# Sixteen weight chunks split in the first dense iteration and two per later one, in place of eight and three

## The chip, the core and the metric

The kernel runs on one core of a Trainium2 chip. The metric is device time in microseconds of one execution. The core has a matrix engine (PE in the profile, with its weight loads as PEld), a vector engine (DVE), a scalar engine (ACT), GpSimd (POOL) and a queue engine that mainly issues transfers (SP). Each runs its own instruction stream in order, and they meet at semaphores.

## What is computed

`x` holds 64 items of 64 tokens with 256 features. Two layers follow each other.

```
# layer 0: one adapter per item
h = gelu(x @ down_W.T + down_b)                     # 256 -> 64
h = h @ expert_W[id].T + expert_b[id] + domain_emb[id]
x = layernorm(h @ up_W.T + up_b + x)
# layer 1: normalise per token, then per item over its tokens, style by subject, two of 8 experts
h = item_norm(layernorm(x)) * gamma[subject] + beta[subject]
gates, idx = top_k(softmax(h @ router_w), 2)        # renormalised gates
y = sum over the two experts of gate * (relu(h @ w1[e] + b1[e]) @ w2[e] + b2[e])
out = x + y
```

The eight experts' `w1` (256 x 1024) and `w2` (1024 x 256) are float32 in memory. The kernel works with each weight as a sum of two float16 numbers, a high and a low part, times 256.

## The kernel before

It has two phases, `dense` and `experts`, one after the other. `experts` runs 39 tiles of gathered rows through the expert matmuls and needs all weights in their two float16 parts (`w_high`, `w_low`) in on-chip memory.

`dense` cuts the 4096 tokens into eight groups of 512 and runs ten iterations, `i.g` = 0 to 9, as a software pipeline: in iteration n the group n is in stage one (`s1`: transposed into features, down, adapter, up, all on PE with ACT copies), group n-1 in stage two (`s2`: the two layer norms of layer 0 and 1 on DVE, ACT and POOL), group n-2 in stage three (`s3`: item norm, router, splitting the rows in high and low parts) and group n-3 in stage four (`s4`: places in the expert queues and the scatter of the rows by POOL). Each engine has its own `body` with these steps in a fixed order, written out by hand, and no engine goes on to the next step before the one ahead is done.

The splitting of the weights is woven into the same iterations. The weights are 32 chunks of 128 x 1024. For a chunk three things happen:

- SP loads it (512 KB) into one of four buffers `stage` (line 364). It waits until the chunk four before it has been cut (`w_low_ready`, line 363).
- ACT makes the high part, `cut_high`, line 642. It waits for the load.
- DVE makes the low part, `cut_low`, line 911, from `stage` and `w_high`. It waits for ACT, and frees the buffer.

`CUTS` says how many chunks belong to each iteration. In iteration 0, ACT and DVE have a body of their own: chunks 0 to 4 stand between the four steps of `copy_selected`, and the rest of the iteration's chunks come in one run at its end, before either engine begins iteration 1:

```python
                        for b in range(SELECTS):
                            cut_high(i, slice(b + 1, b + 2))
                            copy_selected(b)
                        adapted(s1)
                        cut_high(i, slice(SELECTS + 1, None))
                        return
```

In the later iterations ACT makes its high parts at three places among the steps of stage one (the third takes all from the third chunk on), and DVE cuts all low parts of the iteration in one run after `norm_shift` (line 848) and before `best_two` (line 918). Behind that run come `their_experts`, the choice masks, `low` (line 943) and `row_fields`, and then the next iteration's `place_rows` and the moments of its stage two (line 821). `low` waits for `high` (ACT, line 681), which waits for PE's transposes back (line 570), which follow the router's matmuls (line 564); these wait for the item norm (ACT line 667, DVE line 900).

POOL's stream in an iteration: `rstd` of the first norm (lines 437, 439; waits for DVE's moments), three scatters (line 448), two power operations for the item norm (line 463; DVE's `item_scale` at line 880 waits for them), `rstd` of the second norm (DVE's `norm_shift` waits for it), five scatters.

SP's stream in an iteration: in iteration 1 first a store of spare rows and of queue padding, then the iteration's weight loads, then the load of x two groups ahead (waits for `up_done`), then the store of the finished rows `rb`. ACT and DVE wait in iteration 1 also for the small network that makes the style: DVE's `style_layer(1)` (line 792) stands behind its moments, PE's line 503 waits for it and stands ahead of PE's lines 529 and 534, and at the end ACT's `softplus` (lines 633 to 637) is followed by DVE's `item_gammas` (line 814).

Of the kernel before, what the change touches and what calls it, by code (L numbers as in the profile page):

```python
# [53 lines left out]
NONE_ROW = ADAPTERS  # L54
CHUNK = 1024
CHUNKS = 2 * EXPERTS * DC * FF // CHUNK
CUTS = [8, 3, 3, 3, 3, 3, 3, 3, 3, 0]
assert sum(CUTS) == CHUNKS and len(CUTS) == GROUPS + 2
W2_AT = EXPERTS * DC * FF
STAGES = 4  # L60
# [80 lines left out]
def dense(nc, sem, env):  # L141
# [10 lines left out]
    with ExitStack() as ctx:  # L152
# [185 lines left out]
        def chunks(i):  # L338


            start = sum(CUTS[:i.g])
            return [(q, q % STAGES, q // STAGES) for q in range(start, start + CUTS[i.g])]

# [1116 lines left out]
```

## Time and profile before

| | |
|---|---|
| median of 3 runs | 640.93 us (640.7 to 641.24) |
| profiled execution | 642.02 us, its span 640.2 us |
| PE, DVE, ACT, POOL busy | 85%, 63%, 43%, 39% of the span |
| mean granted PE clock | 0.876 of full speed |
| dense phase and tables | 0 to about 239 us of the span |
| expert phase | from about 239 us to the end |
| weight chunks | 32 loads of 512 KB; ACT 1.04 us and DVE 1.22 us for one |

The span is the profiler's time from the first to the last instruction; the execution's own time is 1.8 us longer. A time at a row below is counted from the start of the span. A row with "xN" merges N instructions that follow each other; its duration is theirs together. "idle before" names how long the engine stood still ahead of the row and what ended it.

### The profile page before, as it was taken

How to read it: one execution, taken by the hardware profiler on the slowest of the kernel's cores; microseconds unless marked ns; L12 is line 12 of the kernel's file. 1: busy time of each engine (PE TensorE's matmuls, PEld its weight loads, DVE VectorE, ACT ScalarE, POOL GpSimd, SP SyncE). 2: the span in 40 equal slices, each digit the busy share in tenths (PEclk: the TensorE clock that was granted, in tenths of full speed). 3: DMA queues.
4: the chain of work that ended last, by engine and by line, in shares of the span. 5: the costliest groups of instructions: out<-in, count | busy, mean ns of one | idle time of the engine just before them, and what ended most of it. 6: DMA issues, size and time to landing. Idle time of an engine off the chain costs nothing.

```text
span 640.2 us, 15839 instructions
## 1 busy us (share of the span) xinstructions
PE 542.2 (85%) x4370; PEld 461.7 (72%) x4371; DVE 402.6 (63%) x1431; ACT 278.0 (43%) x628; POOL 247.6 (39%) x208
## 2 busy tenths in 40 slices
PE   5986878888814308999999999999999999999992
PEld 4864665667614306888888888888888888888772
DVE  2566988998896534565656565656565655655571
ACT  2557656666643204343525343434434343434350
POOL 2010388778788520222323333323333323233221
PEclk8689778776865557999999999999999999999997
DMA  9363435565341244433333333333333424232321
GB/s 262 138 193 121 164 129 194 177 196 185 118 153 67 88 154 118 51 42 58 41 58 41 58 47 52 55 44 58 41 58 41 60 39 65 38 44 37 50 33 19
DMA packets 78082, 57.41 MB, mean 90 GB/s; under 512 B 51346, under 2 KB 71699, under 8 KB 77907
## 3 DMA queue, kind: packets, MB, share of 16 engines
q1 hardware_dynamic: 62610, 37.31, 21.4%
q0 software_dynamic: 13296, 17.83, 16.5%
q10 hardware_dynamic: 2146, 1.91, 1.2%
q8 instruction: 14, 0.23, 0.1%
q14 instruction: 16, 0.13, 0.1%
HBM read 23.18 MB, written 24.55 MB: 75 GB/s over the span
## 4 chain that ended last, share of the span: by engine, by line
PE 60%; DMA 1%; issue 1%; POOL 0%; ACT 0%; SPq 0%; DVE 0%; POOLq 0%; DVEq 0%
PE banks L1240 31%; PE banks L1256 29%; DMA out<-yg,token 1%; DMA rT<-queues 1%; POOL out L1205 0%; ACT yg L1304 0%; SPq L1177 0%; DVE yb L1373 0%; POOLq L1214 0%; DVEq L1373 0%; SPq L1179 0%; POOLq L84 0%
## 5 line engine op out<-in xcount | busy, mean ns | idle before, releaser
L1205 POOL DMA_INDIRECT out<-yg,token x71 | 117.0, 1648 | 287.3 <-ACT yg L1304 177.2
L1240 PE MATMUL banks<-rT,w_high 128*128 128x256 f16 (+1 forms) x1248 | 198.0, 266 | 23.9 <-DMA rT<-queues 23.4
L1240 PE MATMUL banks<-rT,w_low 128*128 128x256 f16 (+1 forms) x624 | 163.9, 265 | 0.0
L1256 PE MATMUL banks<-w_high,hid_high 128*128 x568 | 154.9, 273 | 0.8
L1256 PE MATMUL banks<-w_high,hid_low 128*128 x568 | 154.8, 273 | 0.0
L1256 PE MATMUL banks<-w_low,hid_high 128*128 x568 | 154.8, 273 | 0.0
L1288 ACT ACTIVATE hid<-banks,feat 128x256 f32<-128x256 f32 (+1 forms) x312 | 119.4, 455 | 65.6 <-PE banks L1240 52.9
L1240 PEld LDWEIGHTS banks<-rT,w_high 128*128 x1248 | 115.0, 98 | 43.0 <-issue 25.4
L1304 ACT ACTIVATE yg<-yb,gate 128x256 f32<-128x256 f32 x71 | 32.6, 501 | 186.0 <-DVE yb L1373 186.0
L1342 DVE TENSOR_TENSOR hid_low<-hid,hid_high 128x512 f16<-128x512 f32 (+1 forms) x156 | 101.1, 648 | 5.4
L1340 DVE CAST hid_high<-hid 128x512 f16<-128x512 f32 (+1 forms) x156 | 67.8, 434 | 45.4 <-issue 22.8
L1373 DVE SCALAR_TENSOR_TENSOR yb<-banks,b 128x256 f32<-128x256 f32 x71 | 27.2, 420 | 104.4 <-PE banks L1256 102.4
L448 POOL DMA_INDIRECT queues<-h_rows,slot x64 | 72.2, 1128 | 22.8 <-issue 17.4
L1240 PEld LDWEIGHTS banks<-rT,w_low 128*128 x624 | 61.4, 98 | 6.4
L1256 PEld LDWEIGHTS banks<-w_high,hid_high 128*128 128x128 f16 x568 | 55.6, 98 | 8.3 <-issue 1.9
L1256 PEld LDWEIGHTS banks<-w_low,hid_high 128*128 128x128 f16 x568 | 55.6, 98 | 6.4
L1256 PEld LDWEIGHTS banks<-w_high,hid_low 128*128 128x128 f16 x568 | 55.6, 98 | 6.3
L564 PE MATMUL banks<-rw,hT 128*128 128x8 f32 x128 | 21.5, 305 | 31.7 <-ACT hT L667 31.7
L564 PEld LDWEIGHTS banks<-rw,hT 128*128 128x128 f32 x128 | 21.1, 256 | 34.0 <-ACT hT L667 33.9
L911 DVE SCALAR_TENSOR_TENSOR w_low<-stage,w_high 128x1024 f16<-128x1024 f32 x32 | 37.8, 1228 | 2.8 <-ACT w_high L642 2.8
L667 ACT ACTIVATE hT<-hT,aff_c,aff_a 128x64 f32<-128x64 f32 x64 | 22.1, 427 | 33.8 <-DVE aff_c L888 33.8
L642 ACT ACTIVATE w_high<-stage 128x1024 f16<-128x1024 f32 x32 | 33.4, 1053 | 4.3 <-DMA stage<-expert_w 4.3
(179 smaller groups left out, 613.0 us busy)
## 6 DMA issues: line engine op xcount, KB each, us to landing
stage<-expert_w SPq DMA_DIRECT2D x32, 512.0 KB
xb<-x SPq DMA_DIRECT2D x8, 512.0 KB
out<-rb SPq DMA_DIRECT2D x8, 512.0 KB, 3.2
queues<-pad_row SPq DMA_DIRECT2D x5, 260.0 KB
out<-yg,token POOLq DMA_INDIRECT x71, 3.8
queues<-pad_row ACTq DMA_DIRECT2D x4, 260.0 KB
queues<-h_rows,slot POOLq DMA_INDIRECT x64
b<-exp_b SPq DMA_DIRECT2D x1, 1024.0 KB, 5.1
```

The costliest lines, as they stand in the source:

```text
L448: nc.gpsimd.indirect_dma_start(out=queues, out_offset=bass.IndirectOffsetOnAxis(ap=slot[:, i.par, t, k:k + 1], axis=0), in_=h_rows[:, i.pa ...
L564: last = nc.tensor.matmul(ps_lg[:, t, :], hT[:, c, t * P:(t + 1) * P], rw[:, c, :], start=(c == 0), stop=(c == DC - 1))
L642: nc.scalar.activation(w_high[:, bass.ds(q * CHUNK, CHUNK)], stage[:, slot], ACT.Copy, scale=WSCALE).then_inc(w_high_ready, 1)
L911: V.scalar_tensor_tensor(w_low[:, w], stage[:, slot], WSCALE, w_high[:, w], ALU.mult, ALU.subtract).then_inc(w_low_ready, 1)
L1205: nc.gpsimd.indirect_dma_start(out=out, out_offset=bass.IndirectOffsetOnAxis(ap=token[:, i.par, s:s + 1], axis=0), in_=yg[:, i.par, s, :], ...
L1240: last = nc.tensor.matmul(ps_in(i, c), w[:, at], features(i)[:, v, k, :], start=(n == 0), stop=(n == 3 * DC - 1))
L1256: last = nc.tensor.matmul(ps_out(i.par)[:, s, :], v[:, i.par, c, s * P:(s + 1) * P], w[:, at], start=(n == 0), stop=(n == 3 * FC - 1))
L1288: last = nc.scalar.activation(hid[:, c, 0:i.rows], ps_in(i, c), ACT.Relu, scale=1.0 / WSCALE, bias=feat[:, bass.ds(e * FC + (B1 + c), 1)])
L1304: nc.scalar.activation(yg[:, i.par, s, :], yb[:, s, :], ACT.Copy, scale=gate[:, i.par, s:s + 1]).then_inc(gated, 1)
L1340: V.tensor_copy(hid_high[:, i.par, s, r], hid[:, s, r]).then_inc(split_high, 1)
L1342: V.tensor_tensor(hid_low[:, i.par, s, r], hid[:, s, r], hid_high[:, i.par, s, r], ALU.subtract).then_inc(split_low, 1)
L1373: last = V.scalar_tensor_tensor(yb[:, s, :], ps_out(i.par)[:, s, :], 1.0 / WSCALE, b2[:, bass.ds(e * D, D)], ALU.mult, ALU.add)
```

## The change

One line: the numbers of chunks in each iteration. The total stays 32. Iteration 0 gets chunks 0 to 15 (before 0 to 7), iterations 1 to 8 two each (before three). Iteration 9 has none, as before. Nothing else in the source is touched; each engine's stream takes its chunks from `chunks(i)`, which reads `CUTS`.

```diff
 CHUNK = 1024
 CHUNKS = 2 * EXPERTS * DC * FF // CHUNK
-CUTS = [8, 3, 3, 3, 3, 3, 3, 3, 3, 0]
+CUTS = [16, 2, 2, 2, 2, 2, 2, 2, 2, 0]
 assert sum(CUTS) == CHUNKS and len(CUTS) == GROUPS + 2
```

## Rows read from the trace of the kernel before

**Rows 1.** Busy time per engine in stretches; last three: PE clock, DMA share, GB/s.

```profile
0.00:38.89 38.89, 29.99 (x135) 24.35 (x136) 16.98 (x28) 17.59 (x19) 3.52 (x25) 0.69 0.68 204
...
38.89:58.52 19.63, 15.29 (x79) 10.46 (x80) 12.14 (x38) 12.71 (x20) 2.55 (x4) 0.91 0.55 177
...
77.70:98.40 20.70, 16.70 (x83) 13.13 (x84) 17.93 (x85) 12.08 (x23) 16.10 (x13) 0.76 0.46 154
...
179.60:200.30 20.70, 7.30 (x40) 7.13 (x40) 17.82 (x83) 9.42 (x18) 17.16 (x15) 0.52 0.23 82
...
239.00:640.00 401.00, 384.27 (x3576) 338.33 (x3576) 229.31 (x695) 157.01 (x423) 117.00 (x71) 0.98 0.34 50
```

**Rows 2.** Timeline, end of iteration 0: start, duration, engine, line, operation, idle before.

```profile
30.21 1.24 DVE L911 SCALAR_TENSOR_TENSOR w_low<-stage,w_high 128x1024 f16<-128x1024 f32 x1
...
32.98 2.94 ACT L642 ACTIVATE w_high<-stage 128x1024 f16<-128x1024 f32 x3
...
34.05 3.50 DVE L911 SCALAR_TENSOR_TENSOR w_low<-stage,w_high 128x1024 f16<-128x1024 f32 x3 [2.48 <-ACT w_high L642]
...
38.89 1.43 DVE L821 BATCH_NORM_STATS2 stats<-banks 128x6 f32<-128x256 f32 x4 [1.34 <-PE banks L555]
...
39.84 1.08 ACT L649 ACTIVATE xT<-banks 128x512 f32<-128x512 f32 x2 [3.92 <-PE banks L517]
```

**Rows 3.** Timeline: the cut that frees the slot of the seventh load.

```profile
23.40 1.24 DVE L911 SCALAR_TENSOR_TENSOR w_low<-stage,w_high 128x1024 f16<-128x1024 f32 x1
```

**Rows 4.** Windows around loads into `stage`, columns as in rows 1.

```profile
9.00:17.00 8.00, 4.94 (x12) 1.92 (x12) 3.00 (x11) 2.34 (x2) 0.00 (x0) 0.57 1.04 386
...
25.50:27.25 1.75, 1.75 (x10) 1.75 (x9) 1.55 (x2) 1.55 (x2) 0.00 (x0) 0.50 0.86 297
...
36.25:39.75 3.50, 3.50 (x18) 2.76 (x17) 2.16 (x5) 0.00 (x0) 0.00 (x0) 0.86 0.83 282
```

**Rows 5.** Timeline: the same PE work in iterations 0 and 1, and iteration 1's end.

```profile
12.96 1.94 PE L529 MATMUL banks<-ident,item_add 128*64 128x512 f32 x2 [0.53 <-DVE w_high L777]
...
14.69 2.90 PE L534 MATMUL banks<-xT,dw 128*64 128x512 f32 x4
...
41.38 1.07 PE L529 MATMUL banks<-ident,item_add 128*64 128x512 f32 x2
...
42.29 1.88 PE L534 MATMUL banks<-xT,dw 128*64 128x512 f32 x4
...
57.93 0.29 DVE L814 SCALAR_TENSOR_TENSOR item_gamma<-w_high 128x128 f32<-128x128 f32 x1 [5.76 <-ACT w_high L637]
```

**Rows 6.** Timeline: `high` on ACT and `low` on DVE, iterations 2, 3, 7, 8.

```profile
74.24 1.02 ACT L681 ACTIVATE h_rows<-banks 128x1024 f16<-128x1024 f32 x1 [0.73 <-PE banks L570]
...
76.18 1.22 DVE L943 TENSOR_TENSOR h_rows<-banks,h_rows 128x1024 f16<-128x1024 f32 x1
...
95.67 1.02 ACT L681 ACTIVATE h_rows<-banks 128x1024 f16<-128x1024 f32 x1 [1.60 <-PE banks L570]
...
96.86 1.22 DVE L943 TENSOR_TENSOR h_rows<-banks,h_rows 128x1024 f16<-128x1024 f32 x1
...
176.27 1.02 ACT L681 ACTIVATE h_rows<-banks 128x1024 f16<-128x1024 f32 x1 [0.97 <-PE banks L570]
...
178.10 1.22 DVE L943 TENSOR_TENSOR h_rows<-banks,h_rows 128x1024 f16<-128x1024 f32 x1
...
198.93 1.22 DVE L943 TENSOR_TENSOR h_rows<-banks,h_rows 128x1024 f16<-128x1024 f32 x1 [0.51 <-ACT h_rows L681]
```

**Rows 7.** Timeline of POOL: scatters of iteration 3, starts of iterations 4 and 5.

```profile
91.86 2.10 POOL L448 DMA_INDIRECT queues<-h_rows,slot  x1 [0.18 <-issue]
...
96.42 0.96 POOL L448 DMA_INDIRECT queues<-h_rows,slot  x1 [0.30 <-issue]
...
100.31 0.22 POOL L437 TENSOR_SCALAR rs<-mv 128x4 f32<-128x4 f32 x1 [0.40 <-issue]
...
120.65 0.22 POOL L437 TENSOR_SCALAR rs<-mv 128x4 f32<-128x4 f32 x1 [1.50 <-DVE mv L826]
```

## The prediction, made before the changed kernel was run

> **What bounds the kernel now.** I read the page first (shares of the engines), then windows cut at the dense iterations, then the timeline of two iterations, then the waits of POOL and ACT. The windows show two different machines [rows 1]. From 239 us to the end PE is busy 384 of 401 us at clock 0.98: the expert phase is PE's, no weight chunk is split there, and the change can only shift it as a whole. In the dense phase an iteration such as 77.70 to 98.40 takes 20.70 us, of which DVE is busy 17.9; PE (16.7) and POOL (16.1) come close behind. Iteration 0 and iteration 1 are looser: DVE is busy 17.0 of 38.9 us and 12.1 of 19.6 us. What the change takes from the iterations and what it puts at the front are therefore priced separately, each by the wait that ends last there.
>
> **The run at the end of iteration 0.** It now holds chunks 5 to 15 in place of 5 to 7. Today DVE cuts 5, 6, 7 from 34.05 to 37.55, then stands idle 1.34 us until PE is through, and starts iteration 1 at 38.89 with line 821; ACT starts it at 39.84 after 3.92 us idle [rows 2]. The eight new chunks first fill that 1.34 us. Were all data there, they would take DVE 8 x 1.17 = 9.4 us (3.50 us for three [rows 2]) and end at 46.9. But they are not there: four buffers, and a load is issued only when the chunk four before is cut. So each load waits for this chain: chunk cut, load, ACT, DVE. How long is a load? The buffer of the seventh load is free when the cut at 23.40 ends, 24.64 [rows 3], and its bytes move until 27.25 [rows 4]: 2.6 us, with the signal about 2.7. With 1.04 us on ACT, 1.22 on DVE and 0.1 of lags that is 5.1 us for four chunks, 1.28 each, if transfers never collide. If they follow each other closely, bandwidth sets the pace. Two loads back to back took the 3.5 us from 36.25 to 39.75 at 282 GB/s; the start of the kernel, with many transfers queued, moved 386 GB/s for 8 us [rows 4]. For 524,288 bytes that is 1.86 and 1.36 us; I take 1.6 between them, since here two or three loads will be queued, more than in the one window and fewer than in the other.
>
> Step by step: chunk 4 is cut at 31.45 (30.21 + 1.24), so load 8 lands at about 34.2, before ACT is through with 5 to 7 at 35.92 [rows 2]. Load 9 is released by chunk 5's cut at 35.27 (34.05 + 1.22) and lands at 38.0. From there six more loads at 1.6 us: load 15 lands at 47.6, and 2.36 us later (ACT, DVE, lags) its cut ends, at 49.96. That is 11.1 us after 38.89. The bounds: without collisions chunk 9 is cut at 40.4 and chunk 11 at 42.8, load 15 lands 2.7 later and is cut at 47.9, +9.0 us; at 1.86 us a load the run ends at 51.5, +12.6.
>
> A page gives another price for the same thing. The Trainium skill's DMA: Bandwidth & Descriptors, Anatomy of one DMA, has a fit for GpSimd-issued transfers of 2.0 us plus bytes over 436 GB/s. It would give 3.2 us for a load alone and 1.2 us for each further one in a queue; the end of the drain would come to 48.7 us as an estimate from that page, and the whole forecast 1.3 us lower. By that rule, the traced load alone is shorter (2.7) and the traced pair slower (1.86 each at its rate) [rows 3, 4]; these loads are issued by SP, not by GpSimd.
>
> **What stands behind that run.** ACT's features of group 1 (line 649), DVE's moments and style layer 1, and with it PE's lines 503, 529 and 534. PE reads the style layer from DVE, so ACT's being ready a little before DVE gives nothing back. SP's stores of iteration 1, its loads 16 and 17 and the load of x for group 2 wait behind load 15's issue, but that issue comes when chunk 11 is cut, at about 44, and x is wanted only an iteration later: nothing. The adapter's and select's conditions on chunks 16 and up are long met: nothing.
>
> **PE's clock in iteration 1.** PE will have finished the transposes of group 1 soon after 39.84, where ACT's row on them begins [rows 2], and then wait some 11 us for DVE. In iteration 0 after such a pause (mean clock 0.57 from 9 to 17 us [rows 4]) lines 529 and 534 took 1.94 + 2.90 us; in iteration 1 before, at full clock (2.4 GHz), 1.07 + 1.88 [rows 5]. So up to 1.9 us more on a chain that iteration 1 waits for: adapter, up, transposes, softplus. Against it, iteration 1 today has some 3.5 us at half clock (mean clock 0.91 over 19.63 us [rows 1]: 0.09 x 19.63 / 0.5); if they fall elsewhere, up to 1.75 us come back; a longer one costs 1.0 more. I take +1.0 (0 to 2.9).
>
> **The chunk taken from iterations 1 to 8.** DVE saves 1.17 us in each, ACT 1.04. What of it reaches the end?
> Iteration 1: nothing. Behind its cuts DVE idles 5.76 us for ACT's softplus [rows 5].
> Iterations 2 to 8: behind the cuts stand the choice of experts and then `low`, and `low` needs `high` on ACT, which has just come from PE's transposes. The gap between `high`'s end and `low`'s start is all that DVE can move up [rows 6]. In iteration 2: 76.18 - 75.26 - 0.04 of signal = 0.88 us. In iteration 3: 96.86 - 96.69 - 0.04 = 0.13. It grows over the next four, to 0.77 in iteration 7; the five from 3 to 7 add up to 2.7. In iteration 8 `low` already waits 0.51 us for `high`: 0. Together 3.6 us.
> Of the chunks' 8 x 1.17 = 9.4 us, then, 5.8 turns into a wait of DVE for ACT's `high`. Where PE's clock is higher than in this trace `high` comes earlier and the saving can reach the full 1.17 for iterations 2 to 7.
>
> POOL is the next limit. At 100.31 its first operation of iteration 4 follows the last scatter by 0.40 us of pure issue: no slack; at 120.65 it had waited 1.50 for DVE, 1.1 more than that 0.40 [rows 7]. Iteration 7 is like 3, iterations 4, 5, 6 like the second. But scatters that meet a cut take 2.10 us instead of 0.96 [rows 7], 1.1 more, and I expect a scatter that lies under the third cut to give 0.9 of it back when that cut is gone. So POOL allows 0.9 in iterations 3 and 7 and 1.1 in 4 to 6, more than `high` does. At the most then 1.17 + 2 x 0.9 + 3 x 1.1 = 6.3 us. Downwards I allow 2.2, which is what is left if PE's slow stretches fall worse in two of the six.
> The Trainium skill's SBUF — State Buffer (SBUF: two separate sides; Who interferes with whom) says that DVE and GpSimd share a port pair as an exclusive lock, for a DVE instruction with two SBUF inputs only against a GpSimd operation that reads SBUF, and it infers that writing descriptors is spared; spared scatters would mean rival (3) below. By that rule, 2.10 beside 0.96 speaks for a block.
>
> **Sum.** +11.1 (run at the front) + 1.0 (clock) - 3.6 (saved) = +8.5 us. The profiled execution has a span of 640.2 and took 642.02, 1.1 above the median of 640.93; I put the sum on the median: 649.4 us, a profiled span near 648.7.
>
> **Rivals.** What tells a change from none here is about 0.2%, 1.3 us.
> (1) Mild: the drain runs at the chain's own pace (+9.0), clock costs nothing, savings are 6.3: +2.7, 643.6 us. For it: 386 GB/s was reached. Against: the pair at 282 GB/s and the gate at `high` [rows 4, 6]. Cases between +1.3 and +5.5: chance 0.17.
> (2) Heavy: loads at 1.86 us and PE half-clocked through iteration 1: +12.6 + 2.9 - 2.2 = +13.3, 654.2 us. For it: the nearest row for paired loads. Cases above +11.5: 0.14.
> (3) POOL keeps the beat: the scatters get nothing back from the missing cut, iterations 3 and 7 save nothing, and 0.88 + 1.80 = 2.7 us are left: +9.4, 650.3 us. For it: POOL's zero slack at 100.31; against: the long scatter lies exactly under a cut [rows 7]. Chance 0.2, inside the main case's.
> (4) The other side, one mechanism: iteration 1 absorbs the delay. DVE idles 5.76 us there [rows 5]; if the start of iteration 1 on DVE could be late by that without making softplus late, the front would cost 11.1 - 5.8 = 5.3, and with savings of 6.3 and no clock cost the kernel would take 1.0 less, 639.9, or 3.1 less at the lower drain. It decides once absorption and saving together pass the drain's 9.0 to 12.6. Against: softplus is at the end of a chain that begins with DVE's style layer and ACT's features, both behind the run. Faster by over 0.2%: 0.03; within 0.2%, by this or by (1) at its extreme: 0.04.
> That the change does nothing can't be: the counts fix the streams.
> Main case, +5.5 to +11.5: 0.62. A bound under all but (4): DVE's own work in the run costs 46.9 - 38.9 = 8.0 even with all data there, and the iterations give back at most 6.3. Range 644 to 654, which leaves out the ends of (1) and (2).
>
> **What the profile will show.** Right: DVE's line 821 of iteration 1 near 50 us instead of 38.89, ACT and DVE waiting between the cuts of chunks 9 to 15 for `stage`, loads back to back there; iterations 2 to 7 shorter by 0.1 to 0.9 us with new idle time of DVE ahead of line 943, ended by ACT line 681; iteration 1 a little longer at a lower clock; the expert phase of the same length. Wrong: the eight cuts at DVE's own 1.2 us pace, or at 2 us and more; iterations shorter by 1.2 us throughout, with no wait at line 943; iteration 1 shorter by several us; a new wait of POOL or PE in the steady iterations.

## The result, and the profile after

The changed kernel takes 655.36 us (median; 653.11 to 657.84) where the kernel before, on the same chip, takes 640.82 (638.36 to 641.24): a ratio of 1.024, 95% interval 1.018 to 1.029. That is 14.5 us slower. The forecast was 8.5 slower, with 654 as the end of its range; the direction was right and the size was not.

The two profiled executions differ by a little more: span 655.9 against 640.2, 15.7 us. I compare these two, stretch by stretch. First windows of the changed kernel, columns as in [rows 1]: iteration 0, iteration 1, and the expert phase.

```profile
0.00:52.78 52.78, 31.19 (x144) 25.38 (x145) 26.60 (x36) 26.91 (x29) 3.53 (x25) 0.69 0.72 227
52.78:75.25 22.47, 16.86 (x69) 10.33 (x70) 11.21 (x38) 10.80 (x17) 2.55 (x4) 0.74 0.35 114
...
258.00:655.90 397.90, 383.31 (x3574) 337.71 (x3572) 228.71 (x695) 157.25 (x423) 121.51 (x71) 0.98 0.35 50
```

Iteration 0 ends at 52.78 instead of 38.89. Iteration 1 is 22.47 us long instead of 19.63, at a mean clock of 0.74 instead of 0.91, although it holds one chunk less. Iteration 3, also with one chunk less, is longer than before: 21.28 us (20.68 before). An iteration is counted here and below from DVE's start of line 821 on `banks` to the next; iteration 8 ends with the start of line 958, iteration 9 with that of line 1056. The last stretch is the same machine as before: PE busy 383 of 398 us at 0.98. Where the 15.7 us went, by these starts:

| part | forecast | profiled pair |
|---|---|---|
| iteration 0 (start of line 821 in iteration 1) | +11.1 | +13.9 (38.89 to 52.78) |
| iteration 1 | +1.0 | +2.8 (19.63 to 22.47) |
| iterations 2 to 8 | -3.6 | -1.9 (141.77 to 139.90) |
| iteration 9, tables, expert phase | 0 | +0.8 |
| sum | +8.5 | +15.7 |

The last line has nothing of the change in it: iteration 9 takes 19.54 us against 19.52, and from its end to the end of the span it is 421.2 against 420.4, in a stretch whose instructions the edit leaves as they were. In the seventeen profiles of this case that last length lies between 419.1 and 422.0 us, with no order by the counts of chunks, so 0.8 is scatter.

All three terms have the right sign, and all three missed on the same side. How far one pair of profiles can be trusted is seen from the others: iteration 1 starts at 52.8 to 53.6 us in the seven profiles with sixteen chunks at the front, four buffers and SP's order unchanged, and at 38.89, 39.95 and 40.11 in the three with eight. The middle values differ by 13.2 us; the 13.9 of this pair has the earliest start before in it.

Now the end of iteration 0 in the changed kernel, from the timeline; what answers to [rows 2]. ACT first, then DVE.

```profile
33.05 3.88 ACT L642 ACTIVATE w_high<-stage 128x1024 f16<-128x1024 f32 x4
38.83 1.06 ACT L642 ACTIVATE w_high<-stage 128x1024 f16<-128x1024 f32 x1 [1.90 <-DMA stage<-expert_w]
41.09 1.06 ACT L642 ACTIVATE w_high<-stage 128x1024 f16<-128x1024 f32 x1 [1.20 <-DMA stage<-expert_w]
42.37 1.06 ACT L642 ACTIVATE w_high<-stage 128x1024 f16<-128x1024 f32 x1 [0.23 <-DMA stage<-expert_w]
43.65 1.06 ACT L642 ACTIVATE w_high<-stage 128x1024 f16<-128x1024 f32 x1 [0.22 <-DMA stage<-expert_w]
45.51 1.06 ACT L642 ACTIVATE w_high<-stage 128x1024 f16<-128x1024 f32 x1 [0.81 <-DMA stage<-expert_w]
48.04 1.06 ACT L642 ACTIVATE w_high<-stage 128x1024 f16<-128x1024 f32 x1 [1.47 <-DMA stage<-expert_w]
50.55 1.06 ACT L642 ACTIVATE w_high<-stage 128x1024 f16<-128x1024 f32 x1 [1.46 <-DMA stage<-expert_w]
...
34.13 4.63 DVE L911 SCALAR_TENSOR_TENSOR w_low<-stage,w_high 128x1024 f16<-128x1024 f32 x4 [2.49 <-ACT w_high L642]
39.92 1.23 DVE L911 SCALAR_TENSOR_TENSOR w_low<-stage,w_high 128x1024 f16<-128x1024 f32 x1 [1.16 <-ACT w_high L642]
42.17 3.79 DVE L911 SCALAR_TENSOR_TENSOR w_low<-stage,w_high 128x1024 f16<-128x1024 f32 x3 [1.03 <-ACT w_high L642]
46.60 1.23 DVE L911 SCALAR_TENSOR_TENSOR w_low<-stage,w_high 128x1024 f16<-128x1024 f32 x1 [0.64 <-ACT w_high L642]
49.12 1.22 DVE L911 SCALAR_TENSOR_TENSOR w_low<-stage,w_high 128x1024 f16<-128x1024 f32 x1 [1.30 <-ACT w_high L642]
51.64 1.22 DVE L911 SCALAR_TENSOR_TENSOR w_low<-stage,w_high 128x1024 f16<-128x1024 f32 x1 [1.29 <-ACT w_high L642]
52.78 1.41 DVE L821 BATCH_NORM_STATS2 stats<-banks 128x6 f32<-128x256 f32 x4
```

Read it as a ladder. After the first four chunks (5 to 8) each of ACT's rows was released by a load, so its start is the moment at which that load was there: 38.83, 41.09, 42.37, 43.65, 45.51, 48.04, 50.55. The last six steps take 11.72 us, 1.95 each. Against the release, a load takes 3.5 us at first (chunk 5 is cut at 35.3, chunk 9's load is there at 38.83) and 5.9 at last (chunk 11 is cut at 44.65, chunk 15's load is there at 50.55). DVE adds its five waits up to 5.4 us, and all of them are named ACT, which in turn waited for the DMA.

### The profile page after: what moved, and what is told of

It reads as the page before. It is cut to its first block, busy times and chain, and to the rows that moved or that the text cites. A ratio compares the mean times of both kernels' runs of the same rounds, so it can differ in the third digit from the quotient of the medians.

```text
span 655.9 us, 15839 instructions
## 1 busy us (share of the span) xinstructions
PE 539.0 (82%) x4370; PEld 459.1 (70%) x4371; DVE 404.0 (62%) x1431; ACT 279.3 (43%) x628; POOL 247.3 (38%) x208
## 4 chain that ended last, share of the span: by engine, by line
PE 54%; DMA 4%; issue 1%; DVE 1%; POOL 0%; ACT 0%; DVEq 0%; ACTq 0%; POOLq 0%; SPq 0%
PE banks L1240 28%; PE banks L1256 26%; DMA out<-yg,token 3%; DMA rT<-queues 0%; POOL out L1205 0%; DVE yb L1373 0%; DVE hid_high L1340 0%; ACT yg L1304 0%; DVEq L1170 0%; SPq L1177 0%; ACTq L1170 0%; ACT hid L1288 0%; DVE hid_low L1342 0%; DVEq L84 0%; POOLq L84 0%
## 5 line engine op out<-in xcount | busy, mean ns | idle before, releaser
L1205 POOL DMA_INDIRECT out<-yg,token x71 | 121.5, 1711 | 283.7 <-ACT yg L1304 170.4
L448 POOL DMA_INDIRECT queues<-h_rows,slot x64 | 69.7, 1088 | 24.2 <-issue 17.4
L564 PE MATMUL banks<-rw,hT 128*128 128x8 f32 x128 | 23.7, 322 | 36.5 <-ACT hT L667 36.5
L564 PEld LDWEIGHTS banks<-rw,hT 128*128 128x128 f32 x128 | 23.0, 278 | 39.0 <-ACT hT L667 39.0
L437 POOL TENSOR_SCALAR rs<-mv 128x4 f32<-128x4 f32 x16 | 6.7, 418 | 89.6 <-DVE mv L826 89.6
```

Of the source, the lines that this page charges most:

```text
L448: nc.gpsimd.indirect_dma_start(out=queues, out_offset=bass.IndirectOffsetOnAxis(ap=slot[:, i.par, t, k:k + 1], axis=0), in_=h_rows[:, i.pa ...
L564: last = nc.tensor.matmul(ps_lg[:, t, :], hT[:, c, t * P:(t + 1) * P], rw[:, c, :], start=(c == 0), stop=(c == DC - 1))
L1205: nc.gpsimd.indirect_dma_start(out=out, out_offset=bass.IndirectOffsetOnAxis(ap=token[:, i.par, s:s + 1], axis=0), in_=yg[:, i.par, s, :], ...
```

## The experiments

Each is the changed kernel with one edit, if nothing else is said. Ratios are to the kernel before on the same chip, with their 95% intervals.

**The two halves of the change apart.** The first kernel keeps the sixteen at the front and gives iterations 1 to 4 their three chunks back, with one each left for 5 to 8. The second leaves the front at eight, keeps two in iterations 1 to 8, and puts the eight that are left over into iteration 9.

```diff
-CUTS = [16, 2, 2, 2, 2, 2, 2, 2, 2, 0]
+CUTS = [16, 3, 3, 3, 3, 1, 1, 1, 1, 0]   # front sixteen
+CUTS = [8, 2, 2, 2, 2, 2, 2, 2, 2, 8]    # thin without front
```

> Counts 16, 3, 3, 3, 3, 1, 1, 1, 1, 0: the long first run kept, iterations 1 to 4 as before. Theory (front): the run ends near 52.8 us as in the changed kernel (38.9 before), iteration 1 takes about 22.5 us (19.6 before) because PE is at half clock after its wait; time 652 to 657 us. Rival (thin iterations): if a third chunk costs iterations 2 to 4 its whole 1.17 us, they are longer by that than in the changed kernel, in sum 3.5 us over 3 iterations; if PE's clock rules them, their lengths scatter by up to 2 us either way with no such difference.

> Counts 8, 2, 2, 2, 2, 2, 2, 2, 2, 8: the run at the front as before, the steady iterations thin, the eight chunks in the last iteration. Theory (front): line 821 of iteration 1 at 38.9 us, iteration 1 19.6 us long, iterations 2 to 8 together 1 to 4 us shorter than before, the last longer by the eight cuts' 9.4 us less the 3.9 us DVE waits there for the router; time 641 to 645 us. Rival (the extra time is in the thin iterations): they are no shorter, or longer, and iteration 1 is long with a short front too; time over 646 us.

Front sixteen: 655.2 us, ratio 1.0244 (1.0199 to 1.0289), the same as the change. Iteration 1 starts at 53.41 and takes 22.48 us with three chunks, as long as with two: the chunk that the change takes from iteration 1 is worth nothing there, as forecast, and iteration 1 became longer through the front alone. Iterations 2 to 4, with three chunks, take 59.4 us together against 59.1 with two in the changed kernel, and 5 to 7, with one, 57.9 against 60.2: in these two executions the third chunk cost 0.3 us in three iterations, and not the 3.5 that it is on DVE. Thin without front: iteration 1 starts at 40.11 and takes 17.94, and iterations 2 to 8 together 138.93, 2.8 less than before. But it took 654.69 us, 1.0223 (1.0172 to 1.0274), where 641 to 645 was expected, because iteration 9 grew from 19.52 to 34.51 us. Timeline of that iteration, ACT's fifth chunk:

```profile
213.81 1.06 ACT L642 ACTIVATE w_high<-stage 128x1024 f16<-128x1024 f32 x1 [12.98 <-DMA stage<-expert_w]
```

ACT waits 13 us for a load that could not be issued: DVE's first cut of the iteration ends at 208.8 us, SP issues the load then, and ACT's next steps stand behind it. With four buffers that DVE frees only late in an iteration, the fifth chunk of one has to wait like this; the kernel with five in iteration 1, below, shows it too. So this kernel is no clean sum, but its parts carry the reading: no cost in iteration 1, 2.8 us of savings in this execution.

**Fewer at the front.** Twelve in place of sixteen.

```diff
-CUTS = [16, 2, 2, 2, 2, 2, 2, 2, 2, 0]
+CUTS = [12, 3, 3, 3, 3, 2, 2, 2, 2, 0]
```

> Counts 12, 3, 3, 3, 3, 2, 2, 2, 2, 0: half of the change. Theory (the first extra chunk is free in DVE's wait, each further one costs the pace of its load, 1.3 to 2.5 us): line 821 of iteration 1 at 44 to 46 us (38.9 before, 52.8 with sixteen), time 645 to 650. Rival (the run costs by its loads' latency once, not by chunk): it starts at 49 us or more with four extra chunks as well.

649.2 us, 1.0093 (1.0060 to 1.0126). Iteration 1 starts at 45.91, 7.0 us late for four more chunks; the first 1.34 us were free [rows 2], so 8.4 us for four, 2.1 a chunk; sixteen chunks pay (13.9 + 1.3) / 8 = 1.9 a chunk. Iteration 1 takes 22.47 us here too: the whole price of that iteration is there after half of the delay. The time is inside what was expected (645 to 650), and the rival, a latency paid once, would have had the start at 49 or later.

**What makes the run at the front slow: stores or buffers.** SP's queue holds, at the head of iteration 1, a store of spare rows and one of padding. Timeline of SP in the changed kernel; the first row are loads 8 to 15:

```profile
31.54 13.50 SPq L364 DMA_DIRECT2D stage<-expert_w  x8
45.09 0.43 SPq L380 DMA_DIRECT2D out<-hT  x1
45.56 0.43 SPq L382 DMA_DIRECT2D queues<-pad_row  x1
```

Both stores are issued behind load 15, but loads 14 and 15 are on their way then. In this kernel they are issued after the loads of iteration 1 and the load of x; in the next one `stage` has six buffers; the third does both.

```diff
                 def body(i):
-                    if i.g == 1:
-                        sp.wait_ge(cleared_zero, 1)
-                        sp.dma_start(spare_rows, zero_out).then_inc(spare_stored, 16)
-                        sp.wait_ge(rows_numbered, 2)
-                        sp.dma_start(queues[IDLE:IDLE + SLOTS].rearrange("(s p) d -> p s d", p=P),
-                                     bcast(pad_row[:].bitcast(U32), 1, [P, SUB, ROW // 2])).then_inc(filled, 16)
                     load_weights(i, slice(STAGES if i.g == 0 else 0, None))
                     if (s2 := back(i, 1)) is not None:
...
+                        if i.g == 1:
+                            sp.wait_ge(cleared_zero, 1)
+                            sp.dma_start(spare_rows, zero_out).then_inc(spare_stored, 16)
+                            sp.wait_ge(rows_numbered, 2)
+                            sp.dma_start(queues[IDLE:IDLE + SLOTS].rearrange("(s p) d -> p s d", p=P),
+                                         bcast(pad_row[:].bitcast(U32), 1, [P, SUB, ROW // 2])).then_inc(filled, 16)
                         sp.wait_ge(x1_ready, s2.g + 1)
```

```diff
-STAGES = 4
+STAGES = 6
```

> The changed kernel with the store of the spare rows and the queue padding (388 KB) issued after the load of x for group 2 instead of straight behind load 15. Theory (these stores hold up loads 14 and 15, which landed 2.5 us apart against 1.3 before them): the run ends 1 to 2.5 us earlier, near 51 us, and so does the kernel. Rival (the loads' own pace and latency set the run's end): it ends within 0.4 us of 52.8.

> The changed kernel with six buffers in stage instead of four. Theory (the run at the front waits for loads, because a load is only released by the cut four chunks before it): with six released ahead, the loads follow at the 386 GB/s of a full queue, 1.36 us each, DVE ends its run near 49 us instead of 52.8, the time falls by 3 to 5 us. Rival (bandwidth): the loads come no faster than 1.9 us each also with more of them queued; the run ends within 1 us of 52.8.

> The changed kernel with six buffers and with the stores of iteration 1 behind the load of x. Theory (what keeps the front's run from DVE's own pace is only the load's wait for a buffer and these stores): the run ends at 47 to 48 us, against 48.5 with six buffers alone, 46.9 at DVE's own pace, and 52.8 in the changed kernel; 648 to 651 us. Rival (the bytes' bandwidth is a floor of its own): 48.5 or later.

Timelines of DVE, first with the stores behind, then with six buffers (and there one row of ACT), each from the first cut of the run to the moments of iteration 1:

```profile
34.70 4.63 DVE L911 SCALAR_TENSOR_TENSOR w_low<-stage,w_high 128x1024 f16<-128x1024 f32 x4 [2.47 <-ACT w_high L642]
...
52.07 1.42 DVE L821 BATCH_NORM_STATS2 stats<-banks 128x6 f32<-128x256 f32 x4
```

```profile
34.27 9.17 DVE L911 SCALAR_TENSOR_TENSOR w_low<-stage,w_high 128x1024 f16<-128x1024 f32 x8 [2.47 <-ACT w_high L642]
44.30 1.23 DVE L911 SCALAR_TENSOR_TENSOR w_low<-stage,w_high 128x1024 f16<-128x1024 f32 x1 [0.86 <-ACT w_high L642]
46.06 2.50 DVE L911 SCALAR_TENSOR_TENSOR w_low<-stage,w_high 128x1024 f16<-128x1024 f32 x2 [0.54 <-ACT w_high L642]
48.48 1.42 DVE L821 BATCH_NORM_STATS2 stats<-banks 128x6 f32<-128x256 f32 x4
...
41.12 1.06 ACT L642 ACTIVATE w_high<-stage 128x1024 f16<-128x1024 f32 x1 [1.17 <-DMA stage<-expert_w]
```

The run of eleven cuts takes 18.65 us in the changed kernel (34.13 to 52.78), 17.37 with the stores behind (34.70 to 52.07), 14.21 with six buffers (34.27 to 48.48), and 13.83 with both (34.67 to 48.50). By these traces the stores cost 1.3 us with four buffers and 0.4 with six, and the missing buffers 4.4. The same run takes 18.1 to 19.2 us in the seven profiles with four buffers and the stores ahead, so 1.3 can be 0.8 to 1.9, 4.4 can be 3.9 to 5.0, and 0.4 is less than the scatter. With six, eight cuts follow each other at DVE's own pace, and DVE's waits shrink from 5.4 us to 1.4. What the two buffers give is mostly a head start: the first load for which ACT waits in the run is chunk 12's at 41.12, where it was chunk 9's at 38.83; from there to chunk 15's (46.25) the three steps are 1.7 us each, not much under the 1.95 of the changed kernel. In time: 651.61 us, 1.0178 (1.0138 to 1.0218); 650.92, 1.0154 (1.0108 to 1.0200); 651.62, 1.0154 (1.0100 to 1.0208). These intervals overlap each other and that of the change, so the order of the causes is read from the traces and not from the times. Two expectations were missed: with the stores behind, the run ended at 52.07 and not near 51, between theory and rival, and with both edits at 48.50 and not by 48, so that a pace of the transfers beyond buffers and stores is not excluded. Even with every load in time, eleven cuts are 12.9 us of DVE, and eight of them are new: that part no buffer removes.

**PE's clock in iteration 1.** PE stands idle for 14.75 us in the changed kernel before line 503. Timeline of the changed kernel, PE and then DVE; what answers to [rows 5]:

```profile
54.92 0.66 PE L503 MATMUL banks<-w_high 128*128 128x64 f32 x2 [14.75 <-DVE w_high L792]
55.51 1.97 PE L529 MATMUL banks<-ident,item_add 128*64 128x512 f32 x2
57.27 3.62 PE L534 MATMUL banks<-xT,dw 128*64 128x512 f32 x4
...
65.14 1.06 PE L554 MATMUL banks<-uw,dom 65*128 65x256 f32 x2
...
68.59 0.59 PE L555 MATMUL banks<-xb,ident 128*128 128x256 f32 x2
...
61.11 0.28 DVE L798 TENSOR_SCALAR w_high<-banks,ab 64x64 f32<-64x64 f32 x1 [2.65 <-PE banks L503]
61.31 1.39 DVE L821 BATCH_NORM_STATS2 stats<-rb 128x6 f32<-128x256 f32 x4
...
74.66 0.29 DVE L814 SCALAR_TENSOR_TENSOR item_gamma<-w_high 128x128 f32<-128x128 f32 x1 [6.83 <-ACT w_high L637]
```

And DVE before, at the same place:

```profile
44.54 1.39 DVE L821 BATCH_NORM_STATS2 stats<-rb 128x6 f32<-128x256 f32 x4
```

Lines 529 and 534 take 1.97 + 3.62 us in place of 1.07 + 1.88: 2.64 more. The next instruction of PE is the style network's third layer (line 503), and DVE waits 2.65 us for it, where it did not wait before. So DVE reaches its second moments (line 821 on `rb`) 8.53 us after the start of the iteration instead of 5.65, and from there to the end it is 13.94 us against 13.98: the whole loss stands ahead of that line. DVE's wait for ACT's softplus at the end is 6.83 us instead of 5.76 because there is one cut less in front of it. Two kernels give PE work of no use for the wait, 27 and 54 matmuls into a bank that nobody reads.

```diff
                         into_features(s1)
                         if i.g == 1:
+                            for _ in range(27):   # 54 in the second
+                                nc.tensor.matmul(banks[:, 7, 0:P], ident[:], ident[:], start=True, stop=True)
                             style_layer(2)
```

> The changed kernel with 27 more matmuls of the identity by itself on PE, whose result is overwritten, between the transposes of group 1 and line 503, where PE otherwise stands still for about 14 us. Theory (clock): lines 529 and 534 take 1.1 and 1.9 us again instead of 2.0 and 3.6, iteration 1 takes 19.6 to 20.5 us instead of 22.5, the time falls by 1.5 to 3 us. Rival (order): iteration 1 is longer for another wait; it stays at 22 us or more.

> As the run with 27 more matmuls, which ended 6.6 us before PE was wanted again, but with 54, so that PE works on to about 55 us. Theory (clock): lines 529 and 534 take 1.1 + 1.9 us instead of 2.0 + 3.6, iteration 1 falls from 22.5 us to 20.5 or less. Rival (order): both lines stay at half clock or iteration 1 stays above 22 us.

With 27 the work ended at 48.69 and left PE idle for 6.6 us again; it took 655.78 us, 1.0211 (1.0140 to 1.0283), and decides nothing. With 54 (108 instructions in the profile), the timeline of PE, and two windows with the columns of [rows 1]:

```profile
40.83 12.22 PE L612 MATMUL banks<-ident 128*128 128x128 f32 x108
...
55.90 1.97 PE L529 MATMUL banks<-ident,item_add 128*64 128x512 f32 x2
57.66 2.47 PE L534 MATMUL banks<-xT,dw 128*64 128x512 f32 x4
...
53.00:55.00 2.00, 0.05 (x1) 0.00 (x0) 1.97 (x10) 0.66 (x2) 0.00 (x0) 1.00 0.94 348
55.90:57.70 1.80, 1.80 (x4) 0.56 (x4) 1.69 (x6) 0.00 (x0) 0.60 (x1) 0.50 0.02 8
```

PE worked until 53.05, 2.3 us before line 503. The granted clock was still full (1.00) in that pause, where in the changed kernel it was 0.50 from 44 us on, and yet it was 0.50 under line 529, which took 1.97 us as without the matmuls: what was expected, 1.1 and 1.9 us for the two lines, did not come. 655.37 us, 1.0194 (1.0149 to 1.0238). Iteration 1 was 19.59 us long here, but not, as far as the runs tell, for the reason that I had put into the kernel: line 534 and the up projection (lines 554 and 555, 3.7 us instead of 5.4) were faster, and the same shorter iteration came in kernels whose PE stream in iteration 1 is that of the changed kernel. Over all profiles but that of the kernel with five chunks in iteration 1: where the front was long, iteration 1 took 22.4 to 22.5 us in six executions with the up projection at 5.4, one of them the changed kernel profiled again, and 19.6 to 20.2 in five with 3.7; where the front was short, 19.63 twice with 5.4 and 17.9 to 18.0 three times with 3.7. Split at DVE's second moments, the two parts come apart. The first takes 5.65 us with a short front, 8.4 to 8.6 with a long one in the six and 7.3 to 7.9 in the five. The second takes 13.9 to 14.0 us with the up projection at 5.4 and 12.3 with 3.7, whatever the front. So the long front costs iteration 1 some 2.8 us at the one and 1.6 to 2.3 at the other, all of it in the first part, and the clock under the up projection makes another 1.6 to 1.7, which falls one way or the other without the change.

> The changed kernel once more, for one more trace. Theory (whether the half-clock stretch falls into line 554 and 555 of iteration 1 differs from run to run, and makes the two groups of times, 653 and 657 us): if this run takes 652 to 654 us, iteration 1 is 19.6 to 20.2 us long with 3.7 us in lines 554 and 555; if it takes 656 to 658, 22.5 us with 5.4. Rival: the time and iteration 1's length go apart.

The changed kernel again: 659.6 us, one execution; iteration 1 starts at 53.57 and takes 22.40, iterations 2 to 8 take 141.19. The long iteration goes with the long time, as the theory has it, though the time is above the 656 to 658 that I had expected.

**PE's clock in iterations 2 to 8.** First the changed kernel at the gate that the forecast named; timeline of iteration 3:

```profile
106.60 3.59 PE L564 MATMUL banks<-rw,hT 128*128 128x8 f32 x16 [3.32 <-ACT hT L667]
107.44 2.43 DVE L911 SCALAR_TENSOR_TENSOR w_low<-stage,w_high 128x1024 f16<-128x1024 f32 x2
...
110.04 1.95 PE L570 MATMUL banks<-ident,hT 128*128 128x128 f32 x8
...
110.46 0.37 DVE L918 MAX8 top<-lg 128x8 f32<-128x8 f32 x4 [0.59 <-ACT lg L674]
...
112.03 1.02 ACT L681 ACTIVATE h_rows<-banks 128x1024 f16<-128x1024 f32 x1 [1.60 <-PE banks L570]
113.08 1.23 DVE L943 TENSOR_TENSOR h_rows<-banks,h_rows 128x1024 f16<-128x1024 f32 x1 [0.58 <-ACT h_rows L681]
```

DVE is through with its two chunks at 109.87, waits 0.59 us for the router's logits ahead of the choice of experts, and then another 0.58 for `high`; both had waited for PE. The first of these waits is one that the forecast did not have; it is there in iterations 3, 5 and 7 (0.59, 0.68, 0.94 us). What decides is how long PE takes for the router and the transposes back:

| iteration | 2 | 3 | 4 | 5 | 6 | 7 | 8 |
|---|---|---|---|---|---|---|---|
| lines 564 + 570 before, us | 2.9 | 4.8 | 4.6 | 4.4 | 4.3 | 4.2 | 5.5 |
| after, us | 3.0 | 5.5 | 4.1 | 5.5 | 3.6 | 5.2 | 5.5 |
| length before | 19.19 | 20.68 | 20.34 | 20.32 | 20.34 | 20.24 | 20.66 |
| after | 18.09 | 21.28 | 19.68 | 20.83 | 18.86 | 20.51 | 20.65 |

Iterations 2, 4 and 6 save 1.1, 0.7 and 1.5 us; 3, 5 and 7 lose 0.6, 0.5 and 0.3, and they are the ones where PE spends 0.7 to 1.1 us more on these two lines. That is one draw. In seven profiles of kernels with sixteen chunks at the front and two in each later iteration, and with PE's work from iteration 2 on as in the changed kernel, iterations 2 to 8 take 137.7 to 142.1 us in sum, 140.3 in the middle, and 3 to 7 take 99.0 to 103.3; before, they took 141.8 and 101.9. Three kernels put useless matmuls of the same kind ahead of them. The first has eight ahead of the router in each iteration. The second has four to six at three places of iterations 3 to 7. The third is the kernel before with the same.

```diff
                 def route_and_back(i):
+                    pe.wait_ge(act_ready, upto(i.g, 3, GROUPS))
+                    for _ in range(8):
+                        nc.tensor.matmul(banks[:, 6, 0:P], ident[:], ident[:], start=True, stop=True)
                     pe.wait_ge(h_ready, i.g + 1)
                     pe.wait_ge(h_rest_ready, i.g + 1)
-                    pe.wait_ge(act_ready, upto(i.g, 3, GROUPS))
```

```diff
+                def keep_busy(g, n):
+                    for _ in range(n if g >= 3 else 0):
+                        nc.tensor.matmul(banks[:, 4, 0:P], ident[:], ident[:], start=True, stop=True)
...
+                    keep_busy(i.g, 4)
                     pe.wait_ge(act_ready, i.g + 1)
...
+                    keep_busy(i.g, 5)
                     pe.wait_ge(dom_ready, i.g + 1)
...
                 def route_and_back(i):
+                    keep_busy(i.g + 2 if i.g + 2 < GROUPS else 0, 6)
```

> The changed kernel with eight more matmuls of the identity by itself in each iteration ahead of the router's matmuls (line 564), while PE waits for the item norm; their result is overwritten. Theory (at half clock lines 564 and 570 take 5.5 us instead of 3.0, and that holds high, low and so the whole iteration): at full clock in more iterations, iterations 2 to 8 shorten by 2 to 5 us in sum. Rival (the clock is no limit there): their lengths stay, 139.9 us in sum, whatever lines 564 and 570 take.

> The changed kernel with 15 more matmuls of the identity by itself in each of iterations 3 to 7, four ahead of line 546, five ahead of line 554, six ahead of line 564, all where PE waits; their result is overwritten. Theory (PE's half clock, in line 554 and 555 or in 564 and 570, sets how long a thin iteration is): where both groups run at full clock (3.7, 1.95 and 1.1 us) an iteration takes 18.1 to 18.6 us, and iterations 3 to 7 sum to 93 or less instead of 101.2. Rival (another wait): they stay near 20 us each whatever PE's clock.

> The kernel before (8, 3, 3, ...) with the same 15 matmuls in iterations 3 to 7. Theory: at full clock DVE's own chain rules, the third chunk costs its 1.1 us, iterations 3 to 7 sum to 97 to 99 us (101.9 before, and 5 us above the thin ones); the kernel takes 3 to 5 us less than before. Rival (the third chunk is hidden under PE also then): thick and thin iterations are equal within 1 us in sum.

Eight ahead of the router: 654.76 us, 1.0206 (1.0147 to 1.0265). In iterations 2 to 7 the router ran at full speed (1.9 us) and the transposes at or near it (1.1 to 1.7), but iterations 2 to 8 took 139.1 us, hardly less than 139.9, where 2 to 5 us less was expected: the half-clock stretch had gone to the up projection in some iterations, 6.95 us in iteration 4 where full clock makes it 3.7, and made the router late. Three places, with the counts changed (first row, of 93.83 to 190.41, iterations 3 to 7) and with those of before (second row); windows, columns as in [rows 1]:

```profile
93.83:190.41 96.58, 87.48 (x576) 70.60 (x575) 84.23 (x408) 58.72 (x111) 78.62 (x70) 0.92 0.45 153
```

```profile
78.19:180.06 101.87, 89.25 (x578) 70.84 (x576) 89.63 (x411) 64.81 (x117) 80.52 (x69) 0.89 0.53 172
```

With two chunks, the five iterations take 96.6 us instead of the 101.2 of the changed kernel (93 or less was expected; the lowest without these matmuls is 99.0), and the time falls to 651.83 us, 1.0132 (1.0094 to 1.0170). With three, they take 101.9, exactly as before without the matmuls (97 to 99 was expected), and the time is that of before: 641.56, 0.9995 (0.9975 to 1.0016). So a faster PE was worth nothing with three chunks, and 0.9 us an iteration with two (0.5 to 1.3 by the spread above). With three, DVE is busy 89.6 of 101.9 us, and in the timeline of that third kernel (iteration 5) its two larger waits are for POOL:

```profile
128.17 0.17 DVE L887 TENSOR_TENSOR aff_a<-rsT,item_gamma 128x8 f32<-128x8 f32 x1 [1.17 <-POOL rsT L463]
...
132.72 0.16 DVE L855 SCALAR_TENSOR_TENSOR shift<-mv,rs 128x4 f32<-128x4 f32 x1 [0.94 <-POOL rs L439]
```

DVE's work and these answers of POOL set the length there (lines are seven further down in that kernel than in the profile of before, 880 and 848 there). With two chunks PE's router and transposes set it, if they run at half clock. At the higher clock (0.92 and 0.89 of full speed in these windows) a chunk is worth (101.9 - 96.6) / 5 = 1.06 us, nearly DVE's whole 1.17.

**Chunks where DVE waits anyway.** Iteration 1 has DVE idle for 5.8 us, iteration 9 has no chunk, and the front has 1.34 us free. Three kernels use these.

```diff
-CUTS = [16, 2, 2, 2, 2, 2, 2, 2, 2, 0]
+CUTS = [9, 5, 2, 2, 2, 3, 2, 2, 2, 3]   # where DVE waits
+CUTS = [9, 3, 3, 2, 3, 2, 3, 2, 2, 3]   # spread
+STAGES = 6                              # the third: spread, and six buffers
```

> Counts 9, 5, 2, 2, 2, 3, 2, 2, 2, 3: one more chunk than before in iteration 0 (DVE's 1.34 us wait), two more in iteration 1 (5.76 us wait), three in iteration 9 (3.9 us wait), two in most others. Theory (a chunk is free where DVE waits for another engine and costs its load's pace in a run of its own): iteration 1 starts at 38.9 to 39.5 us, is 19.6 to 20.5 long, iteration 9 no longer than 20, the steady ones 2 to 5 us shorter in sum; time 636 to 640 us, faster than both. Rival (the loads with four buffers set the pace wherever the chunks stand): iteration 1 and 9 grow by 2 us or more each, and the time is that of before or above.

> Counts 9, 3, 3, 2, 3, 2, 3, 2, 2, 3: one more in iteration 0 and three in iteration 9, where the run before showed no cost, four fewer in the steady iterations, iteration 1 as before (five chunks there made it 24.4 us). Theory: start of iteration 1 within 1 us of before, iteration 1 17.9 to 19.7, iteration 9 19.6, iterations 2 to 8 1 to 3 us shorter; time 1 to 3 us under before. Rival (the length of the iterations is PE's clock's, whatever DVE has to cut): within 1 us of before.

> Counts 9, 3, 3, 2, 3, 2, 3, 2, 2, 3 with six buffers. Theory (in these counts no cut waits for a load on the way that ends last): same as with four buffers within 1.5 us, 638 to 641 us. Rival (loads still hold something up): 2 us or more faster than with four.

Where DVE waits: 644.73 us, 1.0031 (1.0012 to 1.0050). Three chunks in iteration 9 cost nothing (19.56 us long, 19.52 before), but five in iteration 1 made it 24.38 us in place of 19.63, and the time missed the expected 636 to 640. Timeline of ACT in that iteration, in this kernel and then before:

```profile
51.60 1.06 ACT L642 ACTIVATE w_high<-stage 128x1024 f16<-128x1024 f32 x1 [4.75 <-DMA stage<-expert_w]
52.56 2.06 ACT L687 ACTIVATE nb<-rb,shift,rs 128x256 f32<-128x256 f32 x4
```

```profile
48.02 2.07 ACT L687 ACTIVATE nb<-rb,shift,rs 128x256 f32<-128x256 f32 x4 [0.37 <-DVE shift L848]
```

ACT waits 4.75 us for the fifth chunk's load. Its buffer is free only when DVE has made its first cut of the iteration, at 47.4 us, and ACT's layer norm (line 687), from which the chain to softplus goes on, stands behind it: it starts 15.4 us into the iteration, where before it was 9.1. The up projection ran at 3.7 us here, so the fair comparison is with the 17.95 us of the short iterations above: the two chunks cost 6.4 us. That is the rival of this experiment, the loads with four buffers; whether DVE's idle 5.76 us [rows 5] has room for two cuts once their loads are there, no run shows. Spread: 640.23 us, 0.9974 (0.9949 to 0.9998), some 1.7 us less than before on its chip. Its profile doesn't show where: iterations 2 to 8 took 141.8 us, as before, with four chunks fewer. The same counts with six buffers: 640.68, 0.9998 (0.9975 to 1.0021); iterations 2 to 8 took 143.9 in that execution. That is the best of what was tried, and together they show no gain over the kernel before that I would rely on.

## Why the prediction was right in direction and wrong in size

**The front run: right mechanism, mis-sized, +13.9 for +11.1.** The step that failed first is the load's duration, which I took as 2.7 us alone and 1.6 us apart when queued. The first two points of the ladder were right: chunk 5's cut ends at 35.3 (35.27 forecast), and DVE starts 2.2 us after the last load lands (2.36). Between them, the first load took 3.5 us instead of 2.7, +0.8, and the six steps 1.95 instead of 1.6, +2.1. I had taken 282 and 386 GB/s as the two ends for a queued load [rows 4]; both were windows on bytes in flight, and neither had in it what a load costs from the release of its buffer to the signal that it is there. The 2.7 was the moving of the bytes and a guess for the signal; no weight load of the changed kernel takes less than 3.2 us from issue to landing (median 5.0). A second step put SP's stores at "nothing" because they are issued behind load 15: they move while loads 14 and 15 do, whose steps are 2.5 us, and cost some 1.3 us of the run; the two missing buffers are 4.4. Even my upper bound, 12.6, was passed, by this pair and, barely, by the middle of all starts (13.2).

By the per-byte term of the page DMA: Bandwidth & Descriptors of the Trainium skill (Anatomy of one DMA) each further load in a queue would be 1.2 us, an estimate, and from a fit for transfers that GpSimd issues. No step here is that short: the shortest are two of 1.28, where ACT itself needs 1.06, and the mean is 1.95. The page's price for one alone, also an estimate, 3.2, is what the quickest load here took, where my 2.7 was too short; the load at 50.55 took 5.9 from its release.

**Iteration 1: right mechanism, mis-sized, +2.8 for +1.0.** Lines 529 and 534 lost 2.64 us, and DVE waited 2.65 for what stands behind them; the forecast had up to 1.9 from iteration 0's pair, since it didn't count on 3.62 for line 534. The mistaken step is the credit against it: "if they fall elsewhere, up to 1.75 us come back". The half-clock stretch under the up projection stayed (5.40 us before, 5.41 after), so nothing came back in this execution. In five others of a long front it did, and they stand 2.2 to 2.9 us lower in iteration 1, 1.6 of it from that stretch. The four times of the changed kernel lie in two pairs, near 653.2 and 657.6; both profiles of it (657.84 and 659.6 us) have the long iteration 1 and none of the lower pair was taken, so that this is the cause is likely and not shown.

**The savings: right gate, mis-sized, -1.9 for -3.6.** That `low` would wait for `high`, and that iterations 1 and 8 give nothing, came as forecast (with three chunks or two, iteration 1 is 22.5; iteration 8 is 20.66 and 20.65). Iteration 2 gave 1.10 for 0.88. The 1.9 in sum is the draw of this pair; by the spread over seven profiles it could as well have been 4.0 or nothing. What failed is the step that took the gaps of one trace as the gaps of the next: at 3, 5 and 7 `high` itself came up to a us later, because the router's 16 matmuls took 3.3 to 3.6 us there instead of the 2.2 to 2.9 of before. The lower end of 2.2 allowed two such iterations, and three came. The kernels with PE kept busy support the mechanism from both sides: with fewer slow stretches the thin iterations took 4.6 us less (2.4 less than the lowest of the seven) and the thick ones nothing.

**POOL (rival 3): right that it isn't the limit.** Scatters above 1.8 us fell from nine to six. Timeline of POOL in iteration 7, before and then after; the cuts lie at 173.03 to 176.53 and at 187.03 to 189.39:

```profile
173.09 2.11 POOL L448 DMA_INDIRECT queues<-h_rows,slot  x1 [0.18 <-issue]
175.51 1.85 POOL L448 DMA_INDIRECT queues<-h_rows,slot  x1 [0.31 <-issue]
```

```profile
187.10 2.12 POOL L448 DMA_INDIRECT queues<-h_rows,slot  x1 [0.18 <-issue]
189.52 0.97 POOL L448 DMA_INDIRECT queues<-h_rows,slot  x1 [0.30 <-issue]
```

The second scatter, which lay under the third cut, takes 0.97 us instead of 1.85: the relief of 0.9 that the forecast counted on for iterations 3 and 7. Summed over the two scatters it came in both, and in 8. In 4, 5 and 6, where it counted on none, the two scatters take as long as before or 0.15 us more. The page SBUF — State Buffer of the Trainium skill infers (Who interferes with whom) that writing descriptors is spared a block; the long scatters speak against a scatter that is spared altogether. But not each scatter under a cut is long: in iteration 5 before, one that lies wholly under a cut takes 1.08 us, and what the two share isn't seen.

**Heavy (rival 2), 654.2, was the nearest case**, and each of its three terms was nearly met or passed: 13.9 for 12.6, 2.8 for 2.9, 1.9 for 2.2. Its chance of 0.14 was too low: I treated three doubts as independent and took the middle of each, while two of them, the loads and the clock, had their nearest rows at the heavy end. The mild rival fell (two of six loads came at the chain's own 1.28 us, and the mean was 1.95), and so did the one in which iteration 1 absorbs the delay: DVE's wait for softplus grew from 5.76 to 6.83 us, by the cut that is gone, instead of taking the delay up.

**Open.** Why the up projection of iteration 1 and the router of iterations 3 to 7 run at half clock in one execution and not in another, and why the clock, still full in the pause after 12 us of PE work, was at half under line 529, is not settled by these runs. Nor is whether the loads of the front's run have a pace of their own beside buffers and stores.

## What to carry to other kernels

A run of pieces of work that nothing overlaps is paid at the pace of its loads, and that pace is the time from one release of a buffer to its next (load, high part, low part) over the number of buffers, with what else is in the queue, and not the bytes per second of a busy window: here 7.1 us from chunk 7's cut to chunk 11's and 8.2 from there to chunk 15's, over four. If such a run has to be, more buffers are worth more than a cleaner queue (4.4 us against 1.3 here), mostly because more loads are there when it begins, but the engine's own work in it stays.

Work taken off the busiest engine of a pipeline gives back only the gap up to the next arrival, and if that arrival comes from an engine whose clock changes from run to run, the gap of one trace is not the gap of the next: such a saving should get a wide range, and its low end first.

Idle time of an engine is room for more work only if the inputs of that work can be there, and the engine ahead of it must not stand still for them. Two more chunks in an iteration with 5.8 us of idle DVE cost 6.4 us, since the fifth load had no buffer until DVE's first cut and ACT waited for it with its own chain behind; three in the last iteration were free, and eight there cost 15.

## What was not expected of the hardware

A 512 KB load took 3.5 us from the release of its buffer to its landing at the start of the run and 5.9 at its end, with never more than four in flight; the quickest in the whole kernel took 3.2 from issue to landing. Two stores in the same queue cost some 1.3 us (0.8 to 1.9 by the scatter of the run).

PE's four-row group of line 534 took 1.88 us at full clock and between 2.54 and 3.62 after the long front, in kernels with the same instructions of PE up to there. After 12.2 us of 128-column matmuls the granted clock was 1.00 through a pause of 2.3 us and 0.50 under the two 512-column ones that followed (1.97 us in place of 1.07): work that kept the clock up in the wait did not keep it for what came behind.
